# A graph network on one core: other rests for GpSimd between its gathers

## The reference, cut to what matters

```python
h = relu(layernorm(x))
# first block: attention with 4 heads, and two hops of a mean over neighbours
e = leaky_relu(score_src(h)[src] + score_dst(h)[dst], 0.2)
alpha = segment_softmax(e, dst)
local = segment_sum(alpha * (h @ W_att)[src], dst).mean(heads)
g = h
for _ in range(2):
    g = segment_sum(g[src], dst) / deg
x = x + concat(local, g @ W_g + b_g) @ W_w + b_w
# second block: five layers, h = relu(layernorm(x))
for l in range(5):
    m = leaky(h @ W1[l] + b1[l]) @ W2[l] + b2[l]
    e = leaky(edge_attr @ We1[l] + be1[l]) @ We2[l] + be2[l]
    agg = segment_sum(m[src] * e * dot_scale[l], dst)
    h = layernorm(h + agg * res_w[l]) * ln_g[l] + ln_b[l]
x = x + h
```

## Time and profile before

| | us |
|---|---|
| median of 3 runs | 6910.15 |
| lowest and highest | 6908.07, 6911.17 |
| profiled execution | 6893.8 |
| its span | 6892.0 |
| PE busy | 5232.0 (76%) |
| DVE busy | 5197.8 (75%) |
| POOL busy | 5142.3 (75%) |
| ACT busy | 4110.2 (60%) |

### The profile page before, as it was taken

One profiled execution on the slowest core, in us unless ns is written; L12 is line 12 of the kernel. 1 busy time (PEld: TensorE's weight loads), 2 busy tenths in 40 slices (PEclk: granted clock), 3 DMA queues, 4 the chain that ended last, 5 costly groups with the idle time before them and its releaser, 6 DMA issues.

```text
span 6892.0 us, 140780 instructions
## 1 busy us (share of the span) xinstructions
PE 5232.0 (76%) x51990; PEld 4800.9 (70%) x51995; DVE 5197.8 (75%) x12225; ACT 4110.2 (60%) x6886; POOL 5142.3 (75%) x7040
## 2 busy tenths in 40 slices
PE   7888843333333489998799997999979999799997
PEld 6878732222222388888788887888878888788887
DVE  7877666666666578888688886888878888688887
ACT  4666626555555356666466664666646666466664
POOL 6777777777777467776677775777757777577776
PEclk9999965656555689999899997999979999799998
DMA  4444426777777433333233332333323333233332
GB/s 108 109 106 113 107 69 229 240 245 238 240 236 241 139 85 100 99 97 97 66 97 101 98 98 68 98 99 97 98 67 98 99 96 97 68 96 98 97 99 76
DMA packets 505340, 828.89 MB, mean 120 GB/s; under 512 B 110911, under 2 KB 218038, under 8 KB 491599
## 3 DMA queue, kind: packets, MB, share of 16 engines
q1 hardware_dynamic: 373374, 655.05, 28.3%
q0 software_dynamic: 131280, 164.84, 13.4%
HBM read 385.06 MB, written 434.48 MB: 119 GB/s over the span
## 4 chain that ended last, share of the span: by engine, by line
PE 52%; issue 7%; DVE 4%; ACT 1%; another core or an unknown queue 1%; POOL 1%; DMA 0%; POOLq 0%; DVEq 0%; ACTq 0%
PE psum L1372 45%; PE psum L1386 6%; DVE arena L1773 1%; POOL agg L719 1%; DVE by_lane L1836 0%; ACT gring L1010 0%; PE psum L1298 0%; DVE psum L1819 0%; PE psum L1329 0%; ACT gring L1014 0%; DVE xin L1773 0%; ACT run L995 0%; DVE arena L1790 0%; DMA agg<-rowsg,last_i 0%
## 5 line engine op out<-in xcount | busy, mean ns | idle before, releaser
L712 POOL DMA_INDIRECT gring<-tableh,src_i x2525 | 2480.6, 982 | 863.0 <-issue 587.9
L1372 PE MATMUL psum<-penalty,arena 125*128 125x192 bf16 x25755 | 2474.9, 247 | 248.3 <-issue 227.7
L1372 PEld LDWEIGHTS psum<-penalty,arena 125*128 125x128 bf16 x25755 | 2154.3, 98 | 365.0 <-issue 336.4
L1773 DVE TENSOR_SCALAR arena<-dst_f,node_id 125x768 bf16<-125x768 f16 x4301 | 1762.4, 457 | 0.1
L712 POOL DMA_INDIRECT gring<-table,src_i x1364 | 1384.3, 1015 | 441.2 <-issue 317.1
L703 POOL MEMSET diag<- 128x256 f32 x2916 | 1061.1, 364 | 228.8 <-DMA tableh<-arena 116.7
L985 ACT COPY psum<-diag 128x512 f32<-128x512 f32 x505 | 297.5, 590 | 1338.4 <-issue 765.9
L1813 DVE TENSOR_REDUCE gring<-psum 128x192 f32<-128x576 f32 x505 | 381.9, 756 | 765.9 <-remote 421.2
L1149 PE MATMUL psum<-ident,by_lane 128*128 128x128 f32 x202 | 66.2, 431 | 882.2 <-DMA by_lane<-attr_last 754.6
L1149 PEld LDWEIGHTS psum<-ident,by_lane 128*128 128x128 f32 x202 | 29.1, 203 | 941.1 <-issue 941.1
L923 ACT ACTIVATE arena<-gring,es_w 128x65 f32<-128x65 f32 x1616 | 398.3, 335 | 456.4 <-DMA gring<-table,src_i 445.0
(11 more groups left out here) (280 smaller groups left out, 8748.0 us busy)
## 6 DMA issues: line engine op xcount, KB each, us to landing
rows<-arena SPq DMA_DIRECT2D x101, 1296.0 KB
acts<-arena SPq DMA_DIRECT2D x505, 256.0 KB
arena<-acts SPq DMA_DIRECT2D x505, 256.0 KB
rowsg<-run SPq DMA_DIRECT2D x505, 256.0 KB
dst_f<-pe_src SPq DMA_DIRECT2D x557, 93.8 KB
gring<-tableh,src_i POOLq DMA_INDIRECT x2525
rows<-run SPq DMA_DIRECT2D x101, 256.0 KB
gring<-table,src_i POOLq DMA_INDIRECT x1364
```

What stands on the lines that cost most here:

```text
L712: pool.indirect_dma_start(ring[:, s, k, :], None, table, bass.IndirectOffsetOnAxis(ap=src_i[:, c * K + k:c * K + k + 1], axis=0))\
L1372: ins = mm(found(n)[:, m, :], hot_at(n // 2, j)[:, at:at + P], parts[:, j, :, :].rearrange("q a f -> q (a f)"), start=(j == 0), stop=(j == ...
L1773: ins = ts(hot_at(pair, j), src_row[b], node_id[:, j:j + 1], None, ALU.is_equal)
```

## The change

`pause` gets the number of fills and the tile as arguments, and a new helper `paced` decides before each gather. In the first pass and the layers the helper is called with `burst` = BURST, now 1, and is to do one fill of 128x128 (half the tile). In the second pass `burst` is K = 8, with three fills of 128x256. The counter `issued` no longer counts gathers of the whole program: it is set back to 0 when it equals `burst`, and once by hand before the second pass.

```diff
-BURST = 4
+BURST = 1
@@
-            def pause():
-
-                for _ in range(REST):
-                    pool.memset(rest, 0.0).then_inc(rested, 1)
+            def pause(fills, fill):
+
+                for _ in range(fills):
+                    pool.memset(fill, 0.0).then_inc(rested, 1)
                     rests[0] += 1
                     pool.wait_ge(rested, rests[0])
 
-            def gather_chunk(c, s, table, ring, ready, cols):
+            def paced(burst):
+
+                if issued[0] == burst:
+                    if burst == 1:
+                        pause(1, rest[:, 0:P])
+                    else:
+                        pause(REST, rest)
+                    issued[0] = 0
+                issued[0] += 1
+
+            def gather_chunk(c, s, table, ring, ready, cols, burst=BURST):
                 for k in range(cols):
-                    if issued[0] and issued[0] % BURST == 0:
-                        pause()
-                    issued[0] += 1
+                    paced(burst)
                     pool.indirect_dma_start(ring[:, s, k, :], None, table,
@@
             pool.wait_ge(t2_out, NG * 16)
             settle()
+            issued[0] = 0
             for c in range(CH):
@@
-                gather_chunk(c, c % SL, table2, gather2, g2_ready, K)
+                gather_chunk(c, c % SL, table2, gather2, g2_ready, K, K)
```

## The result

The changed kernel takes 8232.4 us (median of 4 runs, 8177.4 to 8252.6), the kernel before on the same chip 6909.1: a ratio of 1.190, 95% interval 1.184 to 1.197. I had forecast 7052 and a range up to 7330. The side was right, the size was not: +1323 us instead of +142. The experiments then showed something larger: on four of the seven occasions on which kernels ran, the chip was of a kind on which this same change makes the program 8.5% faster. The result first.

A forecast was written before the change was run, and what follows sets the result against it. It took GpSimd's gathers to bound both passes and TensorE the layers, stalled by back-to-back gathers until GpSimd's silence. 6893.8 - 42 (first pass) - 108 (second) + 262 (layers) + 30 (layer starts) + 16 (median) gave 7052 us, range 6620 to 7330.

The forecast's parts named there:

- The counter: Layers: the counter stands at 8 after the second pass, never equals 1, so no fills happen there; 855 in all.
- The second pass: Second pass: 201 rests become 100, each 1.07 us over a plain gap, so 108 us are won.
- The step from four gathers to five: Layers: a fifth gather before the silence lengthens a chunk from 8.12 to 8.66 us, +262 us in all.
- the creep's pace: Layers: TensorE's slowed matmuls before a rest run at 0.31 of full pace, giving 8.79 us a chunk.
- the silence in the layers: Layers: GpSimd's wait on a full ring, once per chunk, clears TensorE's stops as well as fills do.
- The 7.11 us: Layers: TensorE's chunk time once GpSimd has issued its last gather, taken as its pace beside a silent GpSimd.
- signals only in the silence: Layers, rival: each chunk waits for its look-up's signal until 0.95 us after the fifth gather; 9.26 us a chunk, 7336 us, chance 0.09.
- the first pass: First pass: 138 rests go (-167 us), 555 gaps get one narrow fill (+125 us), sum -42 us.
- cover: First pass: VectorE was said to have slack, with 101 chunks of 8.3 us instead of 8.7.
- The layer starts: Start of each layer: 20 gathers go out into an empty ring without a silence, costing 6 us each, +30 us.
- the fills cause the stops: Layers, rival: fills, not gathers, stop TensorE, so the chunk falls to 7.11 us; 6250 us, chance 0.06.

The follow-up runs named there:

- e1: Kernel before with only the second pass changed, one rest of three 128x256 fills per chunk of eight gathers, chip 1: 6626.7 us, ratio 0.983.
- g1: Kernel before with six rest rules by stage (first pass and layer 1 no fills, layer 2 three fills behind every fifth gather), chip 15: 7649.3 us, ratio 1.109.
- j4: No fill anywhere, against the kernel before, chip 1: 5937.7 us, ratio 0.880.
- j3: The changed kernel unaltered, against the kernel before, chip 1: 6171.0 us, ratio 0.915.
- j2: The kernel before, unaltered, run for its trace on chip 1: 6746.0 us.
- j1: Kernel before with two 128x256 fills behind every third gather in first pass and layers, every eighth in second pass, chip 1: 6495.9 us, ratio 0.963.
- e5: The changed kernel unaltered, against the kernel before, chip 8: 6166.0 us, ratio 0.914.

## Why the prediction was wrong

**What held.** The counter was read rightly: no fill in the layers, 855 in all. The kernel before has late signals and stops that GpSimd's silence ends, on the chip of its trace, and the change loses by them. The second pass: -87, forecast -108 (kind one: -118 in e1). The step from four gathers to five, with a silence behind them, has the size that I had worked out: 8.94 measured (g1, layer 2), 8.79 by the creep's pace, of which I took 8.66.

**The step that failed: the silence in the layers.** I wrote that GpSimd's silence, once the ring is full, "clears as well as fills do", and so priced a chunk by the fifth gather alone: +0.54 us, where +2.37 were measured. With rests behind the fifth gather the chunk is 8.94; with the full ring's silence in their place it is 10.50, in the same program on the same chip. That is 1.56 us a chunk, some 780 us in all, that the forecast put at nothing. The 7.11 us from which I argued stood beside a GpSimd that had no gather left to issue, not beside one that starts five more as soon as a slot is free. What the runs show in its place: TensorE is idle 2.1 us a chunk instead of 0.7, nearly all of it stops inside the look-ups, it is busy 8.4 us instead of 7.4 at a granted clock of 0.88 instead of 1.00, and its signals come late besides.

How these hang together is in part argued. A silence that begins with a full ring ends with a freed slot, and the slot is freed by L1828, behind a look-up and a signal that the gathers hold up. The rest of the kernel before is a silence that nobody has to end; GpSimd goes on in it towards slots that are free already. Where the look-up is over before the burst is, this gives the lockstep of the chunk above. The rival "signals only in the silence" had this mechanism, and I gave it 0.09. Its 9.26 was 1.31 too low for that chunk: it had 7.05 from the slot's release to the signal, where 0.78 + 6.00 + 1.45 = 8.23 were measured, and 2.21 for VectorE, where it was 2.34. But it left out TensorE's stops and its lower clock, and by VectorE's waits the look-ups that are not done make up the larger part of what was added. So neither my forecast nor this rival had the whole.

**The same mistake in the first pass.** I priced the fills by GpSimd's issue alone and gave the consumers "cover". By my own reading a rest is what lets signals through, so the narrow fill's half microsecond had to be asked whether it does. It does so only in part: +76 instead of -42. Without any fill that pass takes 1127 us on chip 15 (g1), and 718 on chip 1 (j4).

**The layer starts** were mis-sized, +94 instead of +30: with the ring empty, 20 gathers go out, and the first product comes behind the last of them.

**What no view of the trace could tell.** On chips 1, 6 and 8 the same program has none of the stops. There the kernel before is at GpSimd's pace in the layers (7.96 us a chunk, by the issue of five gathers and 1.25 rests 8.0), VectorE waiting for gathers that land, and whatever shortens GpSimd's work is won until TensorE's 7.11 (j3: 7.10). My rival "the fills cause the stops", 6250 us, is near the changed kernel's time there (6166 to 6171) by luck: it was worked out for the chip with the stops, and on these chips neither fills nor gathers cause any. The Trainium skill, "SBUF — State Buffer", § Who interferes with whom, says that TensorE and ScalarE don't wait for another engine. The traces on these three chips agree (idle 0.0 in j3), those on the chips of the result, 12 and 15 don't (183.3 us of idle in the row above). What holds TensorE there, a port or something else, no run shows.

**Still open.** What differs between the chips. It isn't the granted clock: for the kernel before it is 0.857 to 0.862 over the whole run on 1, 6 and 8, and higher, 0.868 to 0.876, on 12 and 15. That it is the chip and not the hour is argued too: chip 1 ran twice, an hour apart, and was of the first kind both times, but no chip of the second kind is known to have run twice. The kernel before is at 6745 to 6748 us on 1, 6 and 8, at 6826 on 12 and at 6899 on 15, so it is not only yes or no. Nor do I know by which way the gathers hold TensorE; the gathers themselves last as long on both kinds (0.979 us in j2's layers, 0.982 in the first trace). An empty wait as a rest, with no fill in it, was not tried apart from the ring's own.

## What to carry to other kernels

A pause that an engine takes may be what lets other engines' signals through; before you shorten it, look at what ends beside it, and ask of every gap that you leave whether it is long enough for that. A silence that someone must end is no substitute for one that ends by itself: if what ends it is held up until the silence, the two wait for each other, and the price is more than that of one longer burst. And one trace is one chip's: where an interference decides, time both kernels on more than one. For a fleet of both kinds, two fills behind every third gather is the rule to try (layers 7.78 and 7.81 us a chunk; j1 as a whole was timed on the first kind only, 0.963); where all chips are of the first kind, no fills at all (0.880).

## What the runs showed of the hardware

- Two kinds of chip for one program. Kind one (1, 6, 8): 120 gathers in a row in layer 3 of e5, 0.33 us apart at most, no matmul held, the look-up's signal 0.27 us behind the next matmuls' start (median). Kind two (12, 15 and that of the result): beside the same gathers TensorE's matmuls stop (2.1 us a chunk in the result's layer 3) and the signals that it gives come late. There ScalarE's signals pass: in the piece of the changed kernel above, its L1004 ended at 4224.85, amid the gathers, and the transfer that waits for it was issued at 4224.88; of the 458 times that L1004 ended during a gather, none took over 0.03 us.
- On kind two the silence has to go with the gathers: 1.1 us after three costs nothing, after four 0.95 us a chunk; 1.5 after four 0.16 (8.12 in g1 against 7.96 in j2), after five 1.30; 2.4 after five nothing; 0.7 after two 1.67.
- TensorE's granted clock is lowest where it stops most: 0.88 in the layers without rests on kind two, with 2.1 us of idle a chunk, 0.99 with a rest behind the fifth gather and 1.35 us (g1), 1.00 where nothing stops it (j3, layer 3).
- That a kernel is slower by 19% on one chip and faster by 8.5% on another, with under 1% between the runs on either, I had not expected.
